# Layer 0 attention: the two turned scores of a step move to the end of TensorE's order

## The chip, the cores and the metric

The program runs on one NeuronCore of a Trainium2 chip. A core has a matrix engine (TensorE, PE in the rows; its weight loads are PEld), a vector engine (VectorE, DVE), a scalar engine (ScalarE, ACT), GpSimd (POOL) and SyncE (SP), which issues transfers. Each engine takes its own instructions in the order in which the program wrote them, and the engines meet only at semaphores. The metric is device microseconds (us) of one execution of the whole program; lower is better.

## The reference, cut to what matters

Two transformer layers, each an attention and a mixture of experts. The change is in the attention of layer 0 alone: four batches (B = 4) of 512 positions, width 256, 16 heads of 16.

```python
h = _layernorm(x) * (1 + ca) + sa
q, k, v = (proj(w, b) for each)                    # 16 heads of 16
q, k = _apply_rope(q, k, S)
scores = einsum('bhqd,bhkd->bhqk', q, k) / sqrt(16)
attn = softmax(scores, axis=-1)
ctx = einsum('bhqk,bhkd->bhqd', attn, v)
x = x + ga * (ctx.reshape(B, S, D) @ wo.T + bo)
```

## The kernel before, in words

Layer 0's attention (`attention0`) is one software pipeline. Its work is cut into 16 groups G (4 batches, 4 heads in each group), and the loop at the end of the function runs over steps s. In each step it writes what the five engines are to do, engine by engine: `tensor(s)`, `vector(s)`, `scalar(s)`, `gpsimd(s)`, `sync(s)`. That order is written out by hand, and each engine keeps it. A group takes eight steps for each of its parts, and the parts of successive groups overlap:

- **Row scores** (`tensor_scores`, L778): steps 8G to 8G+7. Two matmuls a step, one on rows 0 to 47 and one on rows 64 to 111 of the array. They fill a pair of banks (0 and 1, or 2 and 3). VectorE takes the row maxima (`vector_max`, L790) before the pair is used again two steps later.
- **The shift row**: at step 8G+8 GpSimd splits the maxima, at 8G+9 TensorE turns them (`tensor_nT`, L815, bank 7), at 8G+10 ScalarE copies them out (`scalar_nrow`, L824) and GpSimd issues four small transfers (`gpsimd_nmax`, L834) into rows 48 and 49 of the stack.
- **Turned scores** (`tensor_turned`, L854): steps 8G+13 to 8G+20 (EXP_AT = 13). Two matmuls a step (hh 0 and 1) into banks 4 and 5, each on 50 rows of one half of the array. ScalarE takes the exponential of each (`scalar_exp`, L869). The next step's turned score waits for it, since it uses the same bank.
- **Context** (`tensor_pv`, L883): every second step from 8G+16 (PV_AT = 16), eight matmuls of 32 columns into bank 6. VectorE turns and normalises the sum (L900, L905), GpSimd and ScalarE finish it (L910, L933, L939).
- **The shared bank.** Bank 7 serves everything else, one user at a time (`late = Banks(7, 1)`): the shift row (L815), the rows of the next batch (`tensor_rows`, L1068), its q and k (`tensor_qk`), its v (`tensor_v`), the output projection (`tensor_out`) and its way back (`tensor_back`, L466). The three matmuls of a split product are L126, L127 and L128. All these users fall on odd steps, and context on even steps.

A user of bank 7 first waits until the bank has been read out. Who reads it out, and when:

| user of bank 7 | steps | read out by, and where in that engine's order |
|---|---|---|
| `tensor_nT` | 8G+9 | ScalarE, L824, step + 1, behind that step's two exponentials |
| `tensor_qk`, odd half | 39, 47, 71, 79 | ScalarE, L663, step + 1, behind the exponentials |
| `tensor_v` | 19, 45, 59, 77, 91 | ScalarE, L735, step + 1, behind the exponentials |
| `tensor_rows` | 31, 35, 63, 67 | ScalarE, L1079, the same step, behind the exponentials |
| `tensor_qk`, even half | 43, 51, 75, 83 | VectorE, L674, step + 1, behind that step's maximum |
| `tensor_out` | 53, 55, 85, 87, 117, 119 | VectorE, L997, step + 1, behind the maximum |
| `tensor_back` | 61, 69, 93, 101, 125, 133 | VectorE, L478, step + 1, behind the maximum |

(Steps are those from 13 on, where there are exponentials.) The order of ScalarE within a step is set in `scalar`: first both exponentials, then the shift row, then everything else. ScalarE's halves of q and k (L689, L692) come at steps 45, 53, 77 and 85.

The q and k of a batch go out to DRAM and come back as stacks (SyncE L709, GpSimd L753). The stack of steps 64 to 79 is fetched at steps 51 and 58, and that of steps 96 to 111 at steps 83 and 90. In GpSimd's order the fetch of step 58 (and of 90) stands behind that step's L834.

Of the kernel before, what the change touches and what calls it, by code (L numbers as in the profile page):

```python
# [458 lines left out]
def tensor_residual(k, yT, half, bank, ready):  # L459

    pe, done = k.pe, k.sem("pe_yT")
    pe.wait_ge(*ready)
    for t in range(TT // 2):
        tile = half * (TT // 2) + t
        for i in range(KT):
            mm = pe.transpose(k.psum[:, bank, t * D + i * P:t * D + (i + 1) * P], yT[:, i, tile * P:(tile + 1) * P],  # L466
                              k.ident[:, :])
    mm.then_inc(done.sem, 1)
    return done.up()
# [18 lines left out]
def attention0(k):  # L488
# [7 lines left out]
    with ExitStack() as st:  # L496
# [146 lines left out]
        def tensor_qk(b, i, odd):  # L643
            qk_bank[b, i, odd] = n = g.next()
            if g.free[n]:
                pe.wait_ge(*g.free[n])
            pe.wait_ge(*norm.split_ready[b])
            if (b, odd) == (0, 1):
                pe.wait_ge(*stage_in[1 + i, "lo"])
            col = (2 * i + odd) * P  # L650
            for kt in range(KT):
                mm = k.mm3(psum[:, n, :], w(kt, col, col + P), norm.split(b, kt), kt == 0, kt == KT - 1)
            mm.then_inc(s_qk.sem, 1)
            qk_done[b, i, odd] = s_qk.up()
# [59 lines left out]
        def tensor_v(b, pair):  # L714
            v_bank[b, pair] = n = g.next()
            if g.free[n]:
                pe.wait_ge(*g.free[n])
            pe.wait_ge(*norm.split_ready[b])
            for j in range(2):
                t = 2 * pair + j  # L720
                for kt in range(KT):
                    mm = k.mm3(psum[:, n, j * D:(j + 1) * D], norm.split(b, kt, slice(t * P, (t + 1) * P)),
                               w(kt, 2 * D, 3 * D), kt == 0, kt == KT - 1)
            mm.then_inc(s_v.sem, 1)
            v_done[b, pair] = s_v.up()
            norm.split_free[0] = v_done[b, pair]
# [33 lines left out]
        def of(G, p):  # L760

            return stk[:, :, (G // 2) % NH, 2 * (G % 2) + p]

        def tensor_scores(G, r):
            p, qt = divmod(r, TT)
            u = 8 * G + r
            n = 2 * (u % 2)
            if u >= 2:
                pe.wait_ge(*max_done[u - 2])
            else:  # L770
                for bank in (n, n + 1):
                    pe.wait_ge(*g_first.free[bank])
            if r == 0:
                pe.wait_ge(*stk_in[G // 2])
            pair = of(G, p)
            for hh in range(2):
                rows = slice(64 * hh, 64 * hh + 48)
                mm = pe.matmul(psum[:, n + hh, :], pair[rows, 0, qt * P:(qt + 1) * P], pair[rows, 1, :], start=True,  # L778
                               stop=True)
            mm.then_inc(s_s.sem, 1)  # L780
            s_done[u] = s_s.up()
# [25 lines left out]
        def tensor_nT(G):  # L807
            nT_bank[G] = n = late.next()
            if late.free[n]:
                pe.wait_ge(*late.free[n])  # L810
            if G == 0:
                pe.wait_ge(*ident_r_ready)
            pe.wait_ge(*ncol_ready[G])
            for qt in range(TT):
                mm = pe.matmul(psum[:, n, qt * P:(qt + 1) * P], ncol[:, G % 2, qt, :], ident_r[:, :], start=True,  # L815
                               stop=True)
            mm.then_inc(s_nT.sem, 1)
            nT_done[G] = s_nT.up()
# [23 lines left out]
        def tensor_turned(G, r, hh):  # L842
            kt, p = divmod(r, 2)
            u = 2 * (8 * G + r) + hh
            if u >= 2:
                pe.wait_ge(*e_done[u - 2])
            else:
                pe.wait_ge(*g_first.free[4 + hh])
            if r == 0:
                pe.wait_ge(*nmax_in[G])  # L850
            if u == 0:
                pe.wait_ge(*ones_in)
            pair, rows = of(G, p), slice(64 * hh, 64 * hh + 50)
            pe.matmul(psum[:, 4 + hh, :], pair[rows, 1, kt * P:(kt + 1) * P], pair[rows, 0, :], start=True,  # L854
                      stop=True).then_inc(s_sT.sem, 1)
            sT_done[u] = s_sT.up()
            if G % 2 and r == 7:
                stk_free[G // 2] = sT_done[u]
# [13 lines left out]
        def tensor_pv(G, kt):  # L872
            b, gr = divmod(G, H0 // GROUP0)
            n = TT * G + kt
            if kt == 0:
                if G:
                    pe.wait_ge(*cT_done[G - 1])
                else:
                    pe.wait_ge(*g_first.free[6])
                pe.wait_ge(*v_ready[b])  # L880
            pe.wait_ge(*e_done[4 * n + 3])
            for j in range(GROUP0):
                mm = pe.matmul(psum[32 * j:32 * j + 32, 6, :], v[:, b % NV, kt, GROUP0 * gr + j, :],  # L883
                               et[:, n % NET, j, :], start=(kt == 0), stop=(kt == TT - 1),
                               tile_position=(0, 32 * j), skip_group_check=True)
            mm.then_inc(s_pv.sem, 1)
            pv_done[n] = s_pv.up()
# [99 lines left out]
        def tensor_last_back(half):  # L987
            y_bank[B - 1, half] = n = LAST_BACK[half]
            y_done[B - 1, half] = tensor_residual(k, oT, half, n, ot_done[B - 1])
# [69 lines left out]
        def tensor_rows(b, half):  # L1059
            h_bank[b, half] = n = late.next()  # L1060
            if late.free[n]:
                pe.wait_ge(*late.free[n])
            for t in range(2):
                at, ready = norm.xn_of[b, 2 * half + t]
                pe.wait_ge(*ready)
                for i in range(KT):
                    c = i * 2 * P + t * P
                    mm = pe.transpose(psum[:, n, c:c + P], norm.xn[:, at, i * P:(i + 1) * P], k.ident[:, :])  # L1068
                mm.then_inc(norm.s_xT.sem, 1)
                norm.xn_free[at] = h_turned[b, half] = norm.s_xT.up()  # L1070
# [36 lines left out]
        NCOL_AT, NT_AT, EXP_AT, PV_AT, CTX_AT = 8, 9, 13, 16, 23  # L1107
# [14 lines left out]
        def ahead(s, at):  # L1122

            for b in range(1, B):
                d = s - PER_BATCH * (b - 1) + (SOONER if b == 1 else 0)
                if d in at:
                    yield b, at.index(d)

        def groups(s, at, n=1, every=1):

            for G in range(NG):
                r, rest = divmod(s - 8 * G - at, every)
                if 0 <= r < n and rest == 0:
                    yield G, r

        def tensor(s):
            for G, r in groups(s, EXP_AT, 8):
                tensor_turned(G, r, 0)
            for G, r in groups(s, 0, 8):
                tensor_scores(G, r)  # L1140
            for G, r in groups(s, EXP_AT, 8):
                tensor_turned(G, r, 1)
            for G, kt in groups(s, PV_AT, TT, 2):
                tensor_pv(G, kt)
            for G, r in groups(s, NT_AT):
                tensor_nT(G)
            for b, half in ahead(s, ROWS_AT):
                tensor_rows(b, half)
            for b, j in ahead(s, QK_AT):
                tensor_qk(b, j // 2, 1 - j % 2)  # L1150
            for b, half in ahead(s, V_AT):
                tensor_v(b, half)
            for b in range(B):
                d = s - PER_BATCH * b
                if b < B - 1 and d in OUT_AT:
                    tensor_out(b, OUT_AT.index(d))
                if b < B - 1 and d in BACK_AT:
                    tensor_back(b, BACK_AT.index(d))
                for gr in range(GROUP0):
                    for m in range(KT):  # L1160
                        if b == B - 1 and d == LAST_OUT[gr][m]:
                            tensor_last_out(gr, m)
                if b == B - 1 and d == LAST_BACK_AT:
                    tensor_last_back(0)
                    tensor_last_back(1)

        def vector(s):
            for G, r in groups(s, 0, 8):
# [1850 lines left out]
def adaln_program(nc, ins, out):  # L3019
    with ExitStack() as stack:  # L3020
        k = Kernel(nc, ins, out, stack)
        begin(k)
        attention0(k)
        k.barrier()
        with ExitStack() as early:
# [108 lines left out]
```

## Time and profile before

| | us |
|---|---|
| median of three runs | 1456.45 |
| lowest and highest of them | 1448.93, 1463.96 |
| the profiled execution, whole time | 1450.06 |
| its span, first to last instruction | 1448.8 |
| of it layer 0's attention with turned scores, 70 to 335 | 265 |

### The profile page before, as it was taken

How to read it: one execution, taken by the hardware profiler on the slowest of the kernel's cores; microseconds unless marked ns; L12 is line 12 of the kernel's file. 1: busy time of each engine (PE TensorE's matmuls, PEld its weight loads, DVE VectorE, ACT ScalarE, POOL GpSimd, SP SyncE). 2: the span in 40 equal slices, each digit the busy share in tenths (PEclk: the TensorE clock that was granted, in tenths of full speed). 3: DMA queues.
4: the chain of work that ended last, by engine and by line, in shares of the span. 5: the costliest groups of instructions: out<-in, count | busy, mean ns of one | idle time of the engine just before them, and what ended most of it. 6: DMA issues, size and time to landing. Idle time of an engine off the chain costs nothing.

```text
span 1448.8 us, 22556 instructions
## 1 busy us (share of the span) xinstructions
PE 1294.8 (89%) x6461; PEld 913.3 (63%) x6461; DVE 874.5 (60%) x2649; ACT 780.0 (54%) x1907; POOL 441.0 (30%) x577
## 2 busy tenths in 40 slices
PE   6689799887889998799999999999999986999994
PEld 5334344334556776577777777787777764678773
DVE  5678687753553365765577566666676754543555
ACT  3267575653431545566666556665566643166562
POOL 5344545220344644200000006001410140455553
PEclk9689898987989999899999999999999997999997
DMA  6653617003213553144200001000100018555664
GB/s 219 135 123 84 154 31 151 2 2 149 107 49 99 162 163 100 36 143 140 69 1 1 16 1 60 1 16 1 45 16 16 1 44 326 186 158 156 209 192 139
DMA packets 79207, 133.99 MB, mean 92 GB/s; under 512 B 13788, under 2 KB 52708, under 8 KB 77420
## 3 DMA queue, kind: packets, MB, share of 16 engines
q1 hardware_dynamic: 62128, 92.39, 20.8%
q0 software_dynamic: 15712, 38.25, 9.4%
q10 hardware_dynamic: 1248, 1.90, 0.4%
q8 instruction: 57, 0.93, 0.3%
q14 instruction: 62, 0.51, 0.1%
HBM read 77.20 MB, written 60.00 MB: 95 GB/s over the span
## 4 chain that ended last, share of the span: by engine, by line
PE 69%; DVE 11%; issue 6%; DMA 6%; ACT 4%; POOL 4%; DVEq 0%; SPq 0%; ACTq 0%; POOLq 0%
PE psum L126 9%; PE psum L1984 8%; PE psum L128 8%; PE psum L127 8%; PE psum L2628 7%; PE psum L2674 4%; PE psum L1955 4%; PE psum L2501 4%; PE psum L854 3%; PE psum L883 3%; PE psum L2535 2%; PE psum L2597 1%; PE psum L778 1%; DVE a_nmax L790 1%; POOL slots L1635 1%
## 5 line engine op out<-in xcount | busy, mean ns | idle before, releaser
L790 DVE TENSOR_REDUCE a_nmax<-psum 128x2 f32<-128x1024 f32 x128 | 155.1, 1217 | 66.5 <-PE psum L778 65.5
L869 ACT ACTIVATE a_et<-psum 128x512 f32<-128x512 f32 x256 | 139.0, 594 | 92.0 <-PE psum L854 88.5
L1930 ACT ACTIVATE a_spare<-psum,a_nmax 128x128 f32<-128x128 f32 (+3 forms) x256 | 134.7, 526 | 93.4 <-DVE a_nmax L1919 87.6
L1919 DVE CUSTOM_DVE_ANT_0 psum<-psum,a_spare 128x128 f32<-128x128 f32 (+3 forms) x256 | 126.7, 495 | 79.4 <-PE psum L128 78.6
L2697 POOL DMA_INDIRECT results<-r_fin,r_to x134 | 134.3, 1002 | 123.0 <-ACT r_fin L2689 63.1
L1984 PE MATMUL psum<-a_et,a_v 128*128 128x512 f32 (+3 forms) x512 | 169.5, 433 | 0.0
L2628 PE MATMUL psum<-m_w,m_xT 128*128 x536 | 150.5, 403 | 0.0
L1964 ACT ACTIVATE a_et<-psum 128x128 f32<-128x128 f32 (+3 forms) x256 | 111.6, 436 | 64.2 <-PE psum L1955 60.7
L126 PE MATMUL psum<-a_kT,a_q 128*128 128x128 f32 (+3 forms) x256 | 118.9, 465 | 6.8 <-DVE a_q L1858 5.9
L854 PE MATMUL psum<-a_stk 50*128 50x512 f32 x256 | 109.0, 500 | 15.0 <-ACT a_et L869 12.1
L1955 PE MATMUL psum<-ident,a_spare 128*128 128x128 f32 x640 | 113.5, 275 | 0.6 <-DVE a_spare L1943 0.6
L2674 PE MATMUL psum<-m_w,m_hidT 128*128 (+1 forms) x346 | 103.1, 398 | 8.4 <-DVE m_hidT L2664 7.5
L1943 DVE TENSOR_SCALAR a_spare<-a_spare,a_rinv 128x128 f32<-128x128 f32 (+3 forms) x256 | 103.7, 405 | 9.0
L1984 PEld LDWEIGHTS psum<-a_et,a_v 128*128 128x128 f32 x512 | 95.6, 189 | 18.9
L1941 DVE RECIPROCAL a_rinv<-a_rsum 128x1 f32<-128x1 f32 x256 | 41.6, 163 | 107.7 <-ACT a_spare L1930 100.5
L854 PEld LDWEIGHTS psum<-a_stk 50*128 50x128 f32 x256 | 44.1, 201 | 98.2 <-ACT a_et L869 75.4
L778 PE MATMUL psum<-a_stk 48*128 48x512 f32 x256 | 96.5, 493 | 8.6 <-DMA a_stk<-stacks 6.7
L2645 DVE TENSOR_TENSOR m_hid<-m_silu,psum 128x128 f32<-128x128 f32 (+1 forms) x134 | 40.3, 300 | 103.8 <-ACT m_silu L2638 101.8
L2628 PEld LDWEIGHTS psum<-m_w,m_xT 128*128 128x128 f32 x536 | 91.4, 190 | 13.3
L2689 ACT ACTIVATE r_fin<-psum,r_to 128x256 f32<-128x256 f32 x134 | 63.2, 472 | 45.2 <-PE psum L2674 35.4
L128 PE MATMUL psum<-a_kT,a_q 128*128 128x128 f32 (+3 forms) x256 | 83.7, 327 | 0.0
L1955 PEld LDWEIGHTS psum<-ident,a_spare 128*128 128x128 f32 x640 | 76.7, 141 | 10.9 <-issue 2.4
(326 smaller groups left out, 2940.6 us busy)
## 6 DMA issues: line engine op xcount, KB each, us to landing
r_xs<-slots SPq DMA_DIRECT2D x134, 129.0 KB, 2.3
slots<-empty SPq DMA_DIRECT2D x12, 1290.0 KB, 6.6
m_w<-in_experts SPq DMA_DIRECT2D x16, 768.0 KB, 14.3
stacks<-a_qk SPq DMA_DIRECT2D x32, 256.0 KB, 3.8
a_stk<-stacks POOLq DMA_DIRECT2D x32, 256.0 KB, 7.0
r_shared_hid<-results SPq DMA_DIRECT2D x12, 512.0 KB, 4.6
m_w<-in_experts SPq DMA_DIRECT2D x4, 1216.0 KB, 14.2
a_stk<-stacks POOLq DMA_DIRECT2D x32, 128.0 KB, 6.3
```

Source lines behind the costliest of these rows:

```text
L126: self.pe.matmul(out, lh, rh, start=start, stop=False, skip_group_check=True)
L128: return self.pe.matmul(out, ll, rh, start=False, stop=stop, skip_group_check=True)
L790: dve.tensor_reduce(nmax[:, G % 2, qt, 2 * p:2 * p + 2], psum[:, n:n + 2, :], AX.X, ALU.max, negate=True).then_inc(s_max.sem, 1)
L854: pe.matmul(psum[:, 4 + hh, :], pair[rows, 1, kt * P:(kt + 1) * P], pair[rows, 0, :], start=True, stop=True).then_inc(s_sT.sem, 1)
L869: act.activation(et[:, n % NET, 2 * p + hh, :], psum[:, 4 + hh, :], ACT.Exp).then_inc(s_e.sem, 1)
L1919: dve.tensor_tensor_reduce(psum[:, n, 0:W], psum[:, n, 0:W], mask[:, S - W:S], 1.0, BIG, ALU.add, ALU.min, nmax[:, u % NE, :]).then_inc(s_ ...
L1930: act.activation(e[:, u % NE, 0:W], psum[:, n, 0:W], ACT.Exp, bias=nmax[:, u % NE, :], scale=-1.0, accum_out=rsum[:, u % NE, :]).then_inc( ...
L1955: mm = pe.transpose(psum[:, n, c:c + P], e[:, u % NE, kt * P:(kt + 1) * P], k.ident[:, :])
L1984: mm = pe.matmul(psum[:, n, kt * P:S], v[:, b % 2, kt, h // HPG1 * HD1:(h // HPG1 + 1) * HD1], queries(i, kt), start=(kt == 0), stop=(kt = ...
L2628: mm = pe.matmul(psum[:, n, 0:2 * hid], xT[:, i % NT3, j, :], w[:, bass.ds(start_of[i] + j * 2 * hid, 2 * hid)], start=(j == 0), stop=(j = ...
L2674: mm = pe.matmul(psum[:, n, 0:D], hdT[:, i % NT2, c, :], w[0:CH, bass.ds(start_of[i] + KT * 2 * hid + c * D, D)], start=(c == 0), stop=(c ...
L2697: pool.indirect_dma_start(results[:, :], bass.IndirectOffsetOnAxis(ap=to[:, i % NI, 0:1].bitcast(U32), axis=0), ys[:, o, :], None, bounds_ ...
```

## The change

In `tensor(s)` the two turned scores no longer stand ahead of and behind the row scores. Both are issued at the very end of the step, behind the context and behind whatever uses the shared bank.

```diff
         def tensor(s):
-            for G, r in groups(s, EXP_AT, 8):
-                tensor_turned(G, r, 0)
             for G, r in groups(s, 0, 8):
                 tensor_scores(G, r)
-            for G, r in groups(s, EXP_AT, 8):
-                tensor_turned(G, r, 1)
             for G, kt in groups(s, PV_AT, TT, 2):
                 tensor_pv(G, kt)
             for G, r in groups(s, NT_AT):
...
                 if b == B - 1 and d == LAST_BACK_AT:
                     tensor_last_back(0)
                     tensor_last_back(1)
+            for G, r in groups(s, EXP_AT, 8):
+                tensor_turned(G, r, 0)
+                tensor_turned(G, r, 1)
```

No instruction is added or taken away. The orders of the other four engines, the steps of all parts and every semaphore's count stay as they are.

## Rows read from the trace of the kernel before

**Rows 1.** The page, part 1: busy time, share of the span, instructions, each engine
```profile
PE 1294.8 (89%) x6461; PEld 913.3 (63%) x6461; DVE 874.5 (60%) x2649; ACT 780.0 (54%) x1907; POOL 441.0 (30%) x577
```

**Rows 2.** Stretches: bounds, us, PE, PEld, DVE, ACT, POOL busy, clock, DMA share, GB/s
```profile
70.00:335.00 265.00, 236.92 (x1291) 104.75 (x1292) 185.57 (x220) 170.81 (x320) 105.64 (x180) 0.90 0.34 77
...
186.00:240.00 54.00, 52.53 (x316) 25.54 (x314) 43.48 (x46) 38.31 (x73) 26.38 (x42) 1.00 0.35 89
...
257.00:306.00 49.00, 41.89 (x249) 17.93 (x249) 37.77 (x41) 30.60 (x58) 13.07 (x24) 1.00 0.01 2
```

**Rows 3.** Waits of TensorE, 84 to 310 us: total, times, longest
```profile
PE psum L854 <- ACT a_et L869: 7.4, 15, 0.7
PE psum L778 <- DMA a_stk<-stacks: 6.7, 2, 6.3
```

**Rows 4.** Timeline of steps 78 and 79: start, length, engine, line, count, idle before
```profile
205.38 0.50 PE L854 MATMUL psum<-a_stk 50*128 50x512 f32 x1
205.38 0.72 PE L778 MATMUL psum<-a_stk 48*128 48x512 f32 x2
205.91 1.08 ACT L869 ACTIVATE a_et<-psum 128x512 f32<-128x512 f32 x2 [0.21 <-PE psum L854]
206.05 1.06 PE L883 MATMUL psum<-a_et,a_v 128*32 128x512 f32 x8
207.05 0.50 PE L854 MATMUL psum<-a_stk 50*128 50x512 f32 x1
207.18 0.60 ACT L735 ACTIVATE a_v<-psum 128x512 f32<-128x512 f32 x1 [0.19 <-PE psum L883]
207.83 0.51 PE L126 MATMUL psum<-h_hi_a,a_w_hi 128*128 128x512 f32 x1
209.43 0.49 PE L854 MATMUL psum<-a_stk 50*128 50x512 f32 x1
```

**Rows 5.** Groups by line on ScalarE, 70 to 335 us: busy, mean ns, idle before
```profile
L869 ACT ACTIVATE a_et<-psum 128x512 f32<-128x512 f32 x256 | 139.0, 594 | 92.0 <-PE psum L854 88.5
L824 ACT ACTIVATE a_nrow<-psum 8x512 fp32r<-8x512 f32 x15 | 8.5, 569 | 0.0
L1079 ACT ACTIVATE h_a<-psum,mod 128x256 f32<-128x256 f32 x8 | 4.1, 566 | 0.5 <-PE psum L1068 0.4
L689 ACT ACTIVATE a_qk<-a_turned 128x512 fp32r<-128x512 f32 x5 | 3.2, 633 | 0.0
L735 ACT ACTIVATE a_v<-psum 128x512 f32<-128x512 f32 x5 | 3.0, 602 | 0.4 <-PE psum L883 0.4
L663 ACT ACTIVATE a_turned<-psum,a_bias 128x512 f32<-128x512 f32 x4 | 2.8, 692 | 0.0
```

**Rows 6.** Timeline of steps 107 to 109, where bank 7 has no user
```profile
265.41 0.49 PE L854 MATMUL psum<-a_stk 50*128 50x512 f32 x1
266.65 0.49 PE L854 MATMUL psum<-a_stk 50*128 50x512 f32 x1 [0.50 <-ACT a_et L869]
267.56 1.06 PE L883 MATMUL psum<-a_et,a_v 128*32 128x512 f32 x8
269.16 0.46 PE L854 MATMUL psum<-a_stk 50*128 50x512 f32 x1 [0.53 <-DMA a_stk<-a_nrow]
```

**Rows 7.** Timeline: the first matmul of step 58
```profile
159.44 0.49 PE L854 MATMUL psum<-a_stk 50*128 50x512 f32 x1
```

**Rows 8.** The chain that ended last, from step 58 to step 64: start, length
```profile
161.81 2.10 POOL a_stk L834 x4
...
165.39 11.35 DMA a_stk<-stacks
176.88 0.80 PE psum L778 x2
```

**Rows 9.** Busy time by stretch, as in rows 2, ahead of and behind a clock fall
```profile
239.00:243.00 4.00, 3.07 (x18) 0.97 (x16) 3.85 (x6) 2.65 (x5) 4.00 (x9) 1.00 1.14 223
243.10:256.70 13.60, 13.29 (x53) 4.97 (x52) 7.33 (x8) 6.99 (x13) 4.36 (x8) 0.50 0.56 80
```

## The prediction

> **What bounds the kernel now.** I read the page first. TensorE is busy for 89% of the span, the next engine for 60% [rows 1]. Then the stretches: in layer 0's attention TensorE is busy for 236.92 of 265 us, and in its crowded part, 186 to 240, for 52.53 of 54 at full clock [rows 2]. There VectorE has 43.48 and ScalarE 38.31, so neither can be the bound by its amount of work. From 257 to 306, where no next batch is being prepared, TensorE still has 41.89 of 49 [rows 2]. Third, TensorE's waits: from 84 to 310 us its matmuls wait 7.4 us for exponentials and 6.7 us for stacks, 6.3 of it once [rows 3]. So the stage runs as fast as TensorE works its list off, and every new wait in that list lengthens it unless it falls into a wait that is there anyway.
>
> Last, the timeline, for how a step fits together [rows 4]. Step 78 begins at 205.38 with turned and row scores. The row scores start with the first turned score, so two matmuls on the two halves of the array run side by side. The four take 0.67 us (205.38 to 206.05). Context starts at 206.05 and takes 1.00 us (to 207.05). Step 79's four take 0.67 again, and then the shared bank's user, q of the next batch, starts at 207.83. Two steps with such a user: 209.43 - 205.38 = 4.05 us.
>
> **The change part by part.** Nothing is added or removed, so matmul time changes by nothing. Read in a ring, the order is turned, scores, context, turned, scores, shared user in both kernels: the turned scores of step s now lie next to the row scores of s + 1 instead of those of s. They can still pair (two on one half, two on the other), and there are as many changes between kinds of matmul. Bounds for this: a gain of nothing, since the four already take two slots [rows 4], and a loss of nothing, since each half still has two matmuls. I take 0.
>
> What does change is what the turned scores are behind. ScalarE keeps its order: in step s + 1 first both exponentials, then the read-out of bank 7 that the user of step s filled. Before, the turned scores of s + 1 stood at the head of the step, and the read-out was over by the time that TensorE had done context and the next four: L735 ran from 207.18 to 207.78, and L126 started at 207.83, 0.05 later and at most 0.1 us after it could have [rows 4]. Now these turned scores stand behind context. Let T be when they start. The exponentials start at T + 0.53 (205.91 - 205.38) and take 1.08 [rows 4]. The read-out takes 0.57, 0.60 or 0.69 (L824, L735, L663) [rows 5]. With 0.05 to hand over, the bank is free at T + 0.53 + 1.08 + 0.60 + 0.05 = T + 2.26. TensorE has only the row scores to do beside the turned ones and is at the bank's next user at T + 0.67. The gap is 1.59; an activation begins some 0.1 before the last one ends (two of 0.594 take 1.08), so I take **1.5 us for each user of bank 7 that comes two steps after one read out by ScalarE**. Queued behind the waiting user are the turned scores of its step and the next row scores, hence ScalarE and VectorE as well: nobody catches up for it. A user read out by VectorE costs nothing new: its maximum depends on row scores, and between these and the next user stands the same work as before.
>
> On how strictly TensorE keeps its order: in rows 4 nothing passes L126 while the bank is still being read, which alone doesn't show that nothing could. The Trainium skill ("TensorE: Matmul & The Clock Gate", Architectural detail) says that this engine's queue pulls weight loads ahead but no matmuls. By that rule the sum below stands whole. If turned scores could pass the waiting user, the stalls would go and the time stay as it was.
>
> The sum, with the steps of the users:
>
> - Full stalls at 41, 43, 47, 49, 51 and at 73, 75, 79, 81, 83: 10 x 1.5 = 15.0.
> - At 45 and 77 ScalarE also has halves of q to make (L689 and its twin, 0.63 each [rows 5]), now ahead of the next exponentials and the bank behind them. Up to 1.2 each; half is hidden by context. 2 x 0.6 = 1.2.
> - Stalls at 19, 35, 67. Two of them run at half clock, where TensorE's own work covers more. Between 0.9 and 1.5; 3 x 1.2 = 3.6.
> - After rows of the next batch (33, 65, 69): read out in the same step by two activations of 0.566 [rows 5], free at T + 0.53 + 1.08 + 1.0 = 2.6 against a next user at 0.67 + 1.00 + 0.67 = 2.34. 3 x 0.24 = 0.7.
> - Steps 58 to 64. The row scores of 64 wait for a stack whose fetch stands on GpSimd behind L834, which follows step 58's exponentials: 159.44 to 176.88, 17.4 us [rows 7, 8]. This chain goes on being the limit, so the two stalls at 59 and 61 fall into it and cost nothing. But it now starts one row scores and one context later: 0.67 + 1.00 = 1.7.
> - Steps 90 to 96, the same chain with only a 0.4 us wait at its end (6.7 - 6.3 [rows 3]). Two stalls, 3.0, less that: 2.6.
> - Odd steps without a user (14 of them, most after step 95). Two steps of scores run on end there, limited by exponentials: from one turned score to the next 1.24 us, and 0.91 instead of 0.67 until context [rows 6]. The second turned score is what waits. Row scores now stand behind it instead of ahead: one slot more, 0.24. 14 x 0.24 = 3.4.
>
> Together 15.0 + 1.2 + 3.6 + 0.7 + 1.7 + 2.6 + 3.4 = **28.2 us**.
>
> The shift row's transfers have 1.0 us less cover (one context), and step 109's turned score already waits 0.53 for them [rows 6]. Between 0 and 1.0 for each of the 5 late groups; I take 0: three delays of 0.24 us in each group, already counted, and the later start of the turned scores themselves give most of that cover back.
>
> **The clock.** A stretch with TensorE busy for 3.07 of 4 us was followed by 13.6 us at 0.50, that is 1.2 GHz [rows 9]. Such a stretch costs: 53 matmuls in 13.6 us, against 249 in 49 us or 69 in 13.6 at mostly full clock [rows 2, 9], so 13.6 x (1 - 53/69) = 3.1 us. With stalls, TensorE is busy for about 4.05 of 5.55 us in the crowded part, which is a lower share. How often that makes the clock fall no row tells: 0 to 5 times. I take half a fall, 1.6, as a stall between dense matmuls isn't a long rest. Sum: 28.2 + 1.6 = 29.8.
>
> After the attention everything waits for its result, so the 29.8 us reach the end. The tail (steps 129 to 142) doesn't change: context no longer waits behind turned scores, the last exponentials come as before.
>
> **The rivals.**
>
> *Same, within 1% (0.12).* ScalarE's read-out is late but TensorE's list had slack, or later matmuls pass the waiting one, and only the 3.4 + 1.7 us and a few stalls are left: +0 to +14, some 1460. For it: 7.4 + 6.7 us of waits to fall into [rows 3]. Against it: in the crowded part TensorE idles for only 1.5 of 54 us [rows 2].
>
> *Much slower (0.14).* The ten stalls follow each other, and the clock falls in them: 3 to 6 falls of 3.1 us on top, +39 to +47, some 1497. For it: rows 9. Against it: at half clock TensorE's own 0.67 becomes about 1.2 us and the stalls shrink by the difference.
>
> *Faster (0.03).* The second turned score used to stand behind row scores, which may wait for a maximum or a stack. Now the turned ones go first, and exponentials run through that wait. It would have to take most of 7.4 + 6.7 = 14.1 us [rows 3] and hence give at best 1439. It decides only if ScalarE's read-outs aren't waited for, so if the bank were free by T + 0.67; L126's 0.05 us behind L735 speaks against that [rows 4].
>
> *Forecast (0.71).* Slower by some 30 us.
>
> **How the numbers follow.** 1450.06 + 29.8 = 1479.9 for an execution like the profiled one. The median of the runs shown is 6.4 higher; I go half way, 3.2, and predict 1483. Low end: half of the 28.2 on the profiled time, 1464. High end: the median, 29.8 and five falls, 1456.4 + 29.8 + 15.5 = 1502. Within 1% (14.6 us) is about what a measurement can tell from no change. Slower by over 1%: 0.71 + 0.14 = 0.85. Within 1%: 0.12. Faster by over 1%: 0.03.
>
> **What would show it.** Right: matmuls of bank 7's users (L815, L126, L1068, L466) wait for L824, L735 and L663, about 1.5 us each and some 20 us in all; the attention takes 265 + 30 = 295 us; two steps such as 78 and 79 take 5.5 instead of 4.05; the wait for the stack at step 64 is about 6.3 + 1.7 - 3.0 = 5.0 us. Everything behind the attention keeps its length. Wrong: no waits for ScalarE at bank 7 (then exponentials aren't as late as said), waits of 1.5 us with the attention hardly longer (then another chain was the limit), or more than five stretches at 0.50 in the attention (then the clock is the term that was missed).

## The result, and the profile after

The changed kernel takes 1499.16 us (median of four runs, 1490.23 to 1503.83) against 1456.97 for the kernel before. The ratio is 1.0287, with an interval from 1.0250 to 1.0323: slower by 2.9%. The prediction was 1483, between 1464 and 1502, slower. The direction and the main mechanism hold. The time lies only 3 us below the high end of the range, and the loss of 42 us is well above the 26 that 1483 stood for; in the profiles it is 40.1 against 29.8, a third more.

The profiled execution spans 1488.9 us, 40.1 more than that of the kernel before. These are the stretches of the changed kernel from 45 us on. The columns are the bounds in us, the length, the busy time (and instructions) of PE, PEld, DVE, ACT and POOL, TensorE's granted clock, the transfers' share and GB/s. The second line is layer 0's attention, from the first exponential to the last context:

```profile
45.00:68.50 23.50, 17.98 (x72) 10.34 (x71) 17.95 (x18) 5.02 (x8) 7.02 (x12) 0.86 0.43 98
68.50:367.50 299.00, 249.23 (x1284) 107.49 (x1284) 184.45 (x218) 168.26 (x318) 104.62 (x178) 0.87 0.29 66
367.50:493.80 126.30, 106.75 (x434) 72.35 (x426) 64.63 (x306) 39.23 (x85) 40.23 (x43) 0.83 0.28 103
493.80:1234.00 740.20, 696.64 (x3516) 543.75 (x3516) 459.45 (x1576) 436.44 (x1159) 152.31 (x196) 0.98 0.17 53
1234.00:1488.90 254.90, 215.68 (x1036) 161.92 (x1036) 123.19 (x459) 114.17 (x313) 110.57 (x111) 0.93 0.60 192
```

The same stretches of the kernel before:

```profile
72.00:334.30 262.30, 235.49 (x1286) 104.23 (x1286) 183.61 (x217) 168.82 (x318) 104.67 (x178) 0.90 0.33 76
334.30:460.00 125.70, 104.71 (x434) 71.54 (x427) 63.76 (x307) 39.58 (x85) 40.23 (x43) 0.85 0.28 103
460.00:1200.00 740.00, 694.88 (x3516) 542.81 (x3516) 461.19 (x1576) 436.54 (x1159) 152.17 (x196) 0.99 0.17 53
1200.00:1448.80 248.80, 214.01 (x1036) 160.94 (x1036) 122.69 (x458) 114.25 (x313) 110.69 (x111) 0.93 0.62 197
```

The attention grew by 299.0 - 262.3 = 36.7 us. The two stretches behind it kept their length to within 0.6 us, so the loss goes on to the end whole. The last stretch is 6.1 us longer and the attention began 3.5 us sooner. From the last score matmul of layer 1 to the end it is 274.5 us here and 268.5 before; in the other kernels of this study, one profile of each, it lies between 267.2 and 273.6. The three kernels with TensorE's order of before have 268.1 to 269.2; of the nine with another order eight have more (271.1 to 274.5) and one less (267.2). So it is open whether a part of the 6.1 us goes with the moved order, and nothing shows by what way. It can't be much of the time: with ScalarE's order turned round as well (first experiment), the moved order is as fast as the kernel before.

Now TensorE's longest waits in the attention of the changed kernel, from 70 us on (who waited for whom, total, times, longest):

```profile
PE psum L126 <- ACT a_nrow L824: 9.1, 7, 1.4
PE psum L854 <- DMA a_stk<-a_nrow: 9.0, 5, 4.8
PE psum L815 <- ACT a_turned L663: 5.8, 4, 1.5
PE psum L854 <- ACT a_et L869: 5.7, 13, 0.7
PE psum L126 <- ACT a_v L735: 3.5, 2, 1.8
PE psum L778 <- DMA a_stk<-stacks: 3.2, 1, 3.2
PE psum L466 <- ACT a_v L735: 2.7, 2, 1.4
PE psum L1068 <- ACT a_nrow L824: 2.6, 2, 1.4
```

Five of the eight rows are users of bank 7 that wait for ScalarE's read-out: 9.1 + 5.8 + 3.5 + 2.7 + 2.6 = 23.7 us in 17 waits, 1.39 each. In the kernel before no matmul at bank 7 shows such a wait; its longest rows were those of [rows 3]. The 17 places are those that the prediction names: the ten full stalls, the three at 19, 35 and 67, two in steps 58 to 64, two in steps 90 to 96.

And this is one of them, the same steps 78 and 79 as in [rows 4] (start, length, engine, line, count, idle before; rows between these are left out):

```profile
223.58 0.50 PE L854 MATMUL psum<-a_stk 50*128 50x512 f32 x2
224.24 1.06 PE L883 MATMUL psum<-a_et,a_v 128*32 128x512 f32 x8
225.23 0.57 PE L854 MATMUL psum<-a_stk 50*128 50x512 f32 x2
225.66 0.63 ACT L692 ACTIVATE a_qk<-a_turned 128x512 fp32r<-128x512 f32 x1
226.18 1.08 ACT L869 ACTIVATE a_et<-psum 128x512 f32<-128x512 f32 x2
227.14 0.62 ACT L735 ACTIVATE a_v<-psum 128x512 f32<-128x512 f32 x1
227.81 0.50 PE L126 MATMUL psum<-h_hi_a,a_w_hi 128*128 128x512 f32 x1 [1.77 <-ACT a_v L735]
```

The turned scores of step 78 start at 225.23, behind context. The exponentials follow at 226.18 (here the halves of q are in the way as well), L735 ends at 227.76, and L126 starts 0.05 later, 1.77 us after TensorE could have. Nothing overtakes it. From the turned scores at 223.58 to the next ones of an odd step's end, at 229.63, two steps take 6.05 us instead of the 4.05 of [rows 4].

### The profile page after: what moved, and what is told of

Read it like the earlier page. It is cut to its first block, busy times and chain, and to the rows that moved or that the text cites. A ratio compares the mean times of both kernels' runs of the same rounds, so it can differ in the third digit from the quotient of the medians.

```text
span 1488.9 us, 22556 instructions
## 1 busy us (share of the span) xinstructions
PE 1311.8 (88%) x6461; PEld 917.7 (62%) x6461; DVE 873.1 (59%) x2649; ACT 778.6 (52%) x1907; POOL 442.0 (30%) x577
## 4 chain that ended last, share of the span: by engine, by line
PE 68%; DVE 10%; issue 7%; DMA 6%; ACT 4%; POOL 3%; another core or an unknown queue 1%; SPq 0%; DVEq 0%; POOLq 0%; ACTq 0%
PE psum L126 9%; PE psum L1983 8%; PE psum L128 8%; PE psum L127 8%; PE psum L2627 6%; PE psum L2673 4%; PE psum L1954 4%; PE psum L854 4%; PE psum L883 3%; PE psum L2500 3%; PE psum L2534 2%; PE psum L778 1%; PE psum L2596 1%; ACT a_et L869 1%; DVE a_nmax L790 1%
## 5 line engine op out<-in xcount | busy, mean ns | idle before, releaser
L126 PE MATMUL psum<-a_kT,a_q 128*128 128x128 f32 (+3 forms) x256 | 119.2, 465 | 6.7 <-DVE a_q L1857 5.8
L854 PE MATMUL psum<-a_stk 50*128 50x512 f32 x256 | 85.8, 550 | 15.8 <-DMA a_stk<-a_nrow 9.0
L854 PEld LDWEIGHTS psum<-a_stk 50*128 50x128 f32 x256 | 34.9, 203 | 102.7 <-ACT a_et L869 72.9
L2673 PEld LDWEIGHTS psum<-m_w,m_hidT 128*128 128x128 f32 (+1 forms) x346 | 57.2, 190 | 43.4 <-issue 35.8
```

What stands on the lines that cost most here:

```text
L126: self.pe.matmul(out, lh, rh, start=start, stop=False, skip_group_check=True)
L2673: mm = pe.matmul(psum[:, n, 0:D], hdT[:, i % NT2, c, :], w[0:CH, bass.ds(start_of[i] + KT * 2 * hid + c * D, D)], start=(c == 0), stop=(c ...
```

## Experiments

Theory A: the loss comes from ScalarE's order. Its read-outs of bank 7 stand behind exponentials that now come one context later. Rivals: B, that transfers and the clock make the loss; C, that any place behind bank 7's user is bad; D, that the new neighbours in TensorE's order lose the pairing on the two halves of the array; E, that the long wait for the shift row is only its late copy. "Above before" below is the ratio less 1, times 1453 us, about the median of the kernel before beside these runs.

### Read-outs ahead of the exponentials

```diff
         def scalar(s):
+            for G, r in groups(s, NT_AT + 1):
+                scalar_nrow(G)
+            for b, i in ahead(s, (QK_AT[0] + 1, QK_AT[2] + 1)):
+                scalar_rope(b, i)
+            for b, half in ahead(s, tuple(d + 1 for d in V_AT)):
+                scalar_v(b, half)
             for G, r in groups(s, EXP_AT, 8):
                 scalar_exp(G, r, 0)
                 scalar_exp(G, r, 1)
```

The three loops are gone from where they stood.

> The changed kernel, but in ScalarE's order of a step the three kinds of read-out of bank 7 that belong to the step before (L824 shift row, L663 rope, L735 v) stand ahead of the two exponentials. TensorE's order is that of the changed kernel. Theory A (the read-out waits behind exponentials that are now late): the waits of bank 7's users for ScalarE, 23.7 us in the changed kernel, shrink to under 4 us, and the time comes back to 3 to 12 us above the kernel before. Rival B (transfers and the clock make the loss, and the read-outs only happen to be what ended the waits): the other engines stay late, and the time stays at least 25 us above the kernel before.

Measured: 1449.89 us, ratio 0.9985 (0.9961 to 1.0009), so 2 us below the kernel before, with 1 inside the interval. Its TensorE waits:

```profile
PE psum L854 <- ACT a_et L869: 8.6, 18, 0.8
PE psum L778 <- DMA a_stk<-stacks: 5.4, 1, 5.4
...
PE psum L126 <- ACT a_v L735: 1.6, 2, 0.8
```

Of the 23.7 us, 1.6 are left. They are at steps 47 and 79, where the halves of q are still ahead of L735. TensorE's order was not touched, so the loss of 2.9% hung on what ScalarE did first, and what the order costs by itself is too small for these times to show. Rival B falls: transfers and the clock came back with the stalls (the attention takes 260.5 us, from first exponential to last context). Theory A expected 3 to 12 us too many even then, of which 3.4 were for steps that run on end. That cost is smaller: from context to context around step 107, where no transfer is waited for, it is 3.32 us here and in the changed kernel, against 3.15 in the kernel before.

### Only the shift row's copy ahead

```diff
         def scalar(s):
+            for G, r in groups(s, NT_AT + 1):
+                scalar_nrow(G)
             for G, r in groups(s, EXP_AT, 8):
                 scalar_exp(G, r, 0)
                 scalar_exp(G, r, 1)
-            for G, r in groups(s, NT_AT + 1):
-                scalar_nrow(G)
```

> The changed kernel with only the copy of the shift row (L824) ahead of the exponentials on ScalarE. Theory A: the waits for L824 (9.1 + 2.6 us in the changed kernel) go, those for L663 and L735 (5.8 + 6.2) stay, so 10 to 16 us less than the changed kernel, 24 to 30 above the kernel before. The shift row's transfers are also issued earlier, so the wait of turned scores for them (9.0 us) shrinks by up to 6 if it was lateness, and stays if it is contention with the filling of slots. Rival B: no more than 3 us less.

Measured: 1467.95 us, ratio 1.0097 (1.0067 to 1.0126): 14 us above before, 28 below the changed kernel. I had expected 24 to 30 above. The mechanism held, and these are rows of its waits:

```profile
PE psum L815 <- ACT a_turned L663: 5.9, 4, 1.5
...
PE psum L126 <- ACT a_v L735: 3.6, 2, 1.8
PE psum L466 <- ACT a_v L735: 2.7, 2, 1.4
```

L824 is gone from the list, while the others stand as they were (12.2 us). But the gain was over twice its 11.7 us: the wait of turned scores for the shift row's transfers, 9.0 us, went to nothing too. In the profile the attention takes 277.3 us, 21.7 less than in the changed kernel, which is about these two waits. L824 is ahead of both, the bank and four transfers.

### Behind bank 7's user, ahead of context

```diff
+            for G, r in groups(s, EXP_AT, 8):
+                tensor_turned(G, r, 0)
+                tensor_turned(G, r, 1)
+            for G, kt in groups(s, PV_AT, TT, 2):
+                tensor_pv(G, kt)
```

These stand at the end of `tensor(s)`, in this order, and nowhere else: in a step neither context nor turned scores stand ahead of bank 7's user any longer.

> The turned scores stand behind row scores and behind bank 7's user, but ahead of context. A half of the change: passed on odd steps, not passed on even ones, where exponentials must come soon for the read-out. Theory A (it is context, on the even steps, that must not come first): the exponentials of an even step start some 0.4 us after its row scores, the bank is free at about 2.26 us against a user at 2.0, so a wait of 0.3 us or less for each; 2 to 9 us above the kernel before. Rival C (any place behind bank 7's user is bad): above 20 us.

Measured: 1503.18 us, ratio 1.0319 (1.0259 to 1.0379), 46 us above before. My expectation of 2 to 9 was badly off, though bank 7 behaves as said: its users wait for ScalarE for 1.1 us in all. The loss is elsewhere:

```profile
PE psum L854 <- ACT a_et L869: 29.4, 59, 0.8
...
PE psum L126 <- ACT a_v L735: 1.1, 2, 0.6
```

And two steps of its timeline, with a user of bank 7 (L815) on the odd one:

```profile
191.24 0.50 PE L778 MATMUL psum<-a_stk 48*128 48x512 f32 x2
191.67 0.66 PE L815 MATMUL psum<-a_ident_r,a_ncol 128*128 128x128 f32 x4
192.26 0.50 PE L854 MATMUL psum<-a_stk 50*128 50x512 f32 x2
193.50 0.99 PE L854 MATMUL psum<-a_stk 50*128 50x512 f32 x2 [0.51 <-ACT a_et L869]
194.42 1.06 PE L883 MATMUL psum<-a_et,a_v 128*32 128x512 f32 x8
195.41 0.50 PE L778 MATMUL psum<-a_stk 48*128 48x512 f32 x2
```

The odd step's turned scores come last and the even step's right after its row scores, so only one slot of row scores lies between them. But 1.24 us must (192.26 to 193.50, the same 1.24 as in [rows 6]), since the banks are free only after the exponentials. Behind both there is context and a user of bank 7, where turned scores would have had room. Two steps take 4.17 us; in the kernel before, two with the same user took 3.16 (262.25 to 265.41). In the changed kernel context or bank 7's user lies between two steps' turned scores, but for the odd steps without a user.

### The same, with the read-outs ahead

This is the run above with the edit to `scalar(s)` of the first experiment.

> Turned scores behind bank 7's user and ahead of context, as in the run that came out some 50 us above the kernel before, now with ScalarE's read-outs of bank 7 ahead of the exponentials. Theory F (that run lost its time to exponentials: on even steps its turned scores come only one slot of row scores behind those of the odd step, and 1.24 us must lie between two steps' turned scores): no gain from the read-outs, 35 to 55 us above the kernel before, with the waits of turned scores for exponentials still at about 30 us. Theory A alone (bank 7's read-out): under 15 us above the kernel before.

Measured: 1507.88 us, ratio 1.0393 (1.0348 to 1.0439), 57 us above before, with this wait:

```profile
PE psum L854 <- ACT a_et L869: 28.8, 59, 0.8
```

The read-outs gave nothing here (the expected 35 to 55 was a little low). So this order's loss isn't bank 7's, and rival C falls: a place behind bank 7's user is harmless in the first experiment and costs 3 to 4% here. What counts is the distance between two steps' turned scores.

### Behind context, ahead of bank 7's user

Turned scores stand here and nowhere else:

```diff
             for G, kt in groups(s, PV_AT, TT, 2):
                 tensor_pv(G, kt)
+            for G, r in groups(s, EXP_AT, 8):
+                tensor_turned(G, r, 0)
+                tensor_turned(G, r, 1)
             for G, r in groups(s, NT_AT):
                 tensor_nT(G)
```

> The other half: the turned scores stand behind row scores and context, but ahead of bank 7's user. Theory A: on even steps the exponentials are as late as in the changed kernel. The next step's turned scores now fill part of the wait, but they are bound to the exponentials themselves (1.24 us from one to the next), so that bank 7's user still comes at about 2.3 us instead of 2.34 minus context's 1.0: 15 to 30 us above the kernel before. Rival C: under 8 us.

Measured: 1516.95 us, ratio 1.0441 (1.0392 to 1.0491), 64 us above before, more than twice what I expected. Its largest wait is again the one for exponentials, 24.0 us in 57 waits, with the mirror image of the order above: here the odd step's turned scores follow the even step's with one slot between. The expectation priced that distance as something that fills the stall; it is a loss of its own in every pair of steps, also where bank 7 has no user.

### Both turned scores first

```diff
         def tensor(s):
             for G, r in groups(s, EXP_AT, 8):
                 tensor_turned(G, r, 0)
+                tensor_turned(G, r, 1)
             for G, r in groups(s, 0, 8):
                 tensor_scores(G, r)
-            for G, r in groups(s, EXP_AT, 8):
-                tensor_turned(G, r, 1)
```

> The kernel before with both turned scores at the head of the step, ahead of the row scores: the same neighbours as in the changed kernel (turned, turned, row, row in one run), without the move behind context and bank 7's user. Theory A: the pairing on the two halves of the array stays, only the steps that run on end lose a slot of 0.24 us: 0 to 4 us above the kernel before. Rival D (the order of the four itself costs, by lost pairing): each of 128 steps loses a slot of 0.33 us, and the time is over 15 us higher.

Measured: 1452.13 us, ratio 0.9996 (0.9962 to 1.0029). The neighbours of the changed kernel cost nothing that these times show, to within 5 us either way. Rival D, which asked for over 15 us, falls, and the prediction's 0 for pairing stands.

### The changed kernel with the fillings moved

The slots of the expert layer are filled with zeros by four transfers of 1.29 MB (the last 1.16) from SyncE. In the changed kernel the turned scores of step 37 waited 4.8 us for the shift row. Its chain there (start, length, what):

```profile
110.81 1.58 POOL a_stk L834 x3
112.39 5.94 DMA a_stk<-a_nrow
118.46 0.89 PE psum L854 x2
```

and SyncE's filling at step 36, first in the changed kernel, then in the kernel before, beside GpSimd's issue of the shift row's transfers in the latter:

```profile
111.93 0.38 SPq L195 DMA_DIRECT2D slots<-empty  x1
```

```profile
113.28 2.10 POOL L834 DMA_DIRECT2D a_stk<-a_nrow  x4 [1.88 <-ACT a_nrow L824]
...
115.22 0.38 SPq L195 DMA_DIRECT2D slots<-empty  x1
```

The filling now starts 1.1 us after the first of the four small transfers, where it used to start 1.9 us after, behind all four. The trace tells what that did to each: the two issued at 110.81 and 111.37 landed in 1.64 and 1.59 us, the third, 0.05 us ahead of the filling, in 4.32, and the fourth, 0.46 us behind it, in 5.94. In the kernel before all four landed in 1.59 to 1.65. The edit moves the four fillings to steps where neither they nor a stack is on the way:

```diff
-            j, rest = divmod(s - 12, 24)
-            if rest == 0 and 0 <= j < len(k.fills) and k.fills[j][0] == 0:
-                fill_slots(k, j, s_done[s])
+            if s in (14, 38, 70, 102):
+                fill_slots(k, (14, 38, 70, 102).index(s), s_done[s])
```

> The changed kernel with the four fillings of the slots (1.29 MB each) issued at steps 14, 38, 70 and 102 instead of 12, 36, 60 and 84, so that none is under way together with the shift row's transfers of steps 10 to 13 of a group or with the stack's fetch ahead of steps 64 and 96. Theory A with contention as its second term: the wait of 4.8 us at step 37 shrinks to about 1.5, that at step 64 (3.2) goes; 4 to 9 us less than the changed kernel, 31 to 38 above the kernel before. Rival E (the 4.8 us are only the lateness of the copy L824): no more than 1 us less.

Measured: 1489.26 us, ratio 1.0244 (1.0193 to 1.0294), 35 us above before and 6 below the changed kernel by the ratios, though the two intervals overlap. The profile decides it. Its wait for the shift row:

```profile
PE psum L854 <- DMA a_stk<-a_nrow: 4.1, 4, 1.3
```

The 9.0 us became 4.1 and the longest wait 1.3 instead of 4.8, the wait for the stack at step 64 (3.2 us) is gone, and the attention takes 290.8 instead of 299.0 us. So the long wait was contention with the filling (rival E falls). The other four waits stay at their steps and at their size (29, 101, 109 and 125, 0.7 to 1.3 us each); they are the lateness of L824, since the copy ahead took them to nothing in the second experiment.

### The fillings moved in the kernel before, and all edits together

The same four lines in the kernel before; then in the run with turned scores last and read-outs ahead; then in the kernel before with read-outs ahead.

> The kernel before with the same four fillings moved. If the 11.35 us that the stack's fetch takes ahead of step 64 are contention with the filling that starts 0.3 us after it, the wait of 6.3 us there shrinks by 3 to 6 us, and the kernel is 3 to 8 us faster than before (the clock's fall behind that wait may go too). If the fetch takes that long by itself, no difference.

> Turned scores last, ScalarE's read-outs of bank 7 ahead of the exponentials, and the fillings moved: all that was found put together. By theory A the stalls are gone, and the wait for the stack at step 64 (5.4 us with the read-outs ahead) goes as well: 5 to 12 us faster than the kernel before. Rival: the wait for the stack is set by GpSimd's order, not by the filling, and it is within 3 us of the run with the read-outs ahead.

> The kernel before (TensorE's order untouched) with ScalarE's read-outs of bank 7 ahead of the exponentials and the four fillings of the slots moved. If TensorE's order in itself is neutral, this is within 3 us of the same two edits on top of the changed order (ratio 0.9942): 5 to 12 us faster than the kernel before. If the changed order gives something that the late read-out had covered (turned scores ahead of row scores that wait), this is 4 us or more behind that one.

| | median us | ratio to before | interval | attention in the profile |
|---|---|---|---|---|
| fillings moved | 1449.76 | 0.9955 | 0.9921 to 0.9989 | 259.9 |
| and turned scores last, read-outs ahead | 1446.29 | 0.9942 | 0.9914 to 0.9970 | 250.1 |
| and read-outs ahead, TensorE's order as before | 1440.42 | 0.9955 | 0.9928 to 0.9983 | 250.3 |

(The first two medians and the third come from different sets of runs; each ratio is to the kernel before of its own set.) The second row's kernel is faster than both kernels of this case, by 0.6%. In it TensorE's matmuls wait neither for a stack nor, but for 0.2 us, for the shift row, and the clock stays up:

```profile
70.30:320.40 250.10, 231.73 (x1280) 101.80 (x1284) 182.98 (x217) 167.75 (x319) 105.10 (x178) 0.96 0.36 79
```

The three ratios can't be told apart, and the attention takes the same 250 us in both orders of TensorE. So turned scores last give nothing by themselves, and by the ratios most of the gain is the fillings'. By how much the read-outs add to it these runs don't settle: the attentions say 10 us, the ratios nothing, and the granted clock (0.90 with the fillings alone, 0.96 here) is a part of the 10. The read-outs ahead alone, in TensorE's order of before, were not run. In the run with the fillings alone the 6.7 us of waits for stacks [rows 3] shrank to 0.7 and yet the attention got only 2.4 us shorter: waits for the shift row rose from 2.2 to 5.0 us, with two new ones of 1.7 us at steps 69 and 101; why they came is open.

## Why the prediction was right, and where it was short

**The mechanism.** It named the queue (ScalarE's exponentials ahead of the read-out), the places and the price of one stall. Seventeen waits of 1.39 us on average came, against 1.5 in the sum. With the queue's order turned round the loss is gone. The turned scores don't pass the waiting matmul: at steps 78 and 79 TensorE stands still for 1.77 us, though the exponential that frees bank 4 for the next turned score was over at 226.78, 1.03 us before L126 started. The Trainium skill ("TensorE: Matmul & The Clock Gate", Step-by-step: what each phase is for) says that the queue pulls weight loads ahead while matmuls keep the program's order, and by that rule the sum was the right one. As a rule for every matmul the trace of the kernel before contradicts it: in 113 of the 128 steps the second matmul of the row scores, the one that signals their semaphore, starts ahead of the first, which uses the other half of the array (205.39 against 205.72 us in step 78). So what is shown here is that nothing passed a matmul that waits for its bank, and the waiting ones of bank 7 take all 128 rows of the array.

**The sum, stretch by stretch.** The table takes the start of the row scores (L778) of a step in both profiles and shows how the difference grows between two steps.

| steps | forecast, without the clock | measured | what the trace shows |
|---|---|---|---|
| 12 to 32 | 2.2 | -1.0 | 7 us less at half clock at the start |
| 32 to 40 | 1.7 | 7.0 | the filling in front of the shift row, step 37 |
| 40 to 58 | 8.1 | 9.6 | the row of stalls |
| 58 to 64 | 1.7 | -0.7 | chain 2 us shorter from L834 on (below) |
| 64 to 84 | 9.8 | 14.1 | the second row of stalls, more at half clock |
| 84 to 96 | 2.8 | 1.9 | |
| 96 to 104 | 0.5 | -3.0 | the clock's fall of [rows 9] is missing |
| 104 to 116 | 1.0 | 4.7 | half clock instead |
| 116 to the last context | 0.5 | 3.7 | |

**The terms that were mis-sized.**

- *The shift row's transfers, taken at 0.* They cost 9.0 - 2.2 = 6.8 us. The prediction saw the 1 us of lost cover, gave a range of 0 to 1 for each of five groups and chose the low end, on the grounds that other delays give the cover back; they didn't. And it didn't look at what else SyncE's queue would send in that moment. Moving the fillings gives 4.9 us back, the copy ahead gives all.
- *The clock, taken at 1.6.* The granted clock of the attention is 0.87 against 0.90. At 0.50, that is 1.2 GHz, it runs for 77 us against 55, so 22 us more. At the prediction's own price (3.1 us in 13.6) they cost 5.1 us, an estimate. In the crowded part, where TensorE is the bound, the price is probably higher; no run isolates it. One of the prediction's own signs of being wrong came: more than five stretches at 0.50 in the attention. There are nine, of 1.9 to 20.5 us, against four of 13.6 before. This stretch is mostly at 1.2 GHz:

```profile
298.00:319.00 21.00, 20.48 (x70) 8.97 (x70) 9.96 (x10) 8.44 (x16) 4.36 (x8) 0.53 0.01 2
```

- *The 3.4 us of steps that run on end.* The cost is real but was put too high. From context to context at full clock it is 3.15 us around steps 27 and 107 in the kernel before and 3.34 and 3.32 here, 0.17 to 0.19 more and not 0.24; around steps 23 and 103, where context waits for VectorE, it is 3.67 and 3.73 before and 3.68 and 3.74 here. By that it is under 2 us in all, an estimate. The 0.7 us for rows of the next batch shouldn't have been there: no matmul waits for L1079.
- *The halves of q.* They were put at 0.6 us each behind the users at 45 and 77. What they cost is at the next users, 47 and 79: waits of 1.76 and 1.77 us against 1.39 on average.
- *Steps 58 to 64.* The stack's chain went on being the limit, and the two stalls fell into it, as predicted. It starts 1.3 us later in the step, not 1.7 (from the first row scores of step 58 to L834 3.7 us against 2.4), and this was made good: in [rows 8] 15.1 us lie from L834 to the row scores of step 64, here 13.0 (L834 at 175.65, scores at 188.66), as the stack's transfer in the chain took 9.30 us instead of 11.35. The wait is 3.2 us, against 5.0 forecast.

By waits: 23.7 us at bank 7, 6.8 more for the shift row, 3.5 less for stacks (6.7 to 3.2) and 5.4 less of turned scores for exponentials (12.1 to 6.7, the first steps included) make 21.6 of the 36.7 us. The rows of the stretches say the same in another way. TensorE's idle time in the attention grew from 26.8 to 49.8 us, by 23.0; the other 13.7 are busy time (235.49 to 249.23) of the same matmuls. Against the run with the read-outs ahead, which has the very same order on TensorE, busy time is 12.0 us longer (237.21 there) with 35 us more at half clock. So a large part of the 13.7 is probably the clock, more than the 5.1 at the prediction's price, and a part are the steps that run on end; how it divides is not shown.

**The rivals.** "Much slower" was half right. By its number the result belongs to it: +40 us in the profile, in its +39 to +47, and 1499 us against its 1497. The clock did fall more often too, but in shorter falls, by 22 us of half clock over the stage, which is under two of the falls of 13.6 us and not 3 to 6; and a part of the loss is the wait for the shift row, which is in neither sum. That the range still holds the result is in part luck: its high end has five falls in it, and what took their place was other terms. "Faster" had its mechanism too, fewer waits of turned scores (12.1 to 6.7 us), under a larger loss.

## What to carry to other kernels

When instructions move within one engine's order, write down for every other engine what is queued behind the result that now comes later. Here it was a 0.6 us copy behind two exponentials, and it cost 2.9%; turning that engine's own order round made the move free, as far as the times can tell. A result that two things wait for (L824: a bank and four transfers) pays twice. And where an engine-to-engine loop has a least distance (from one step's turned scores to the next some 1.2 us, and in no kernel here under 1.14), any order that leaves less work than that between two of them loses in that turn: the two orders that did so cost 3.2 and 4.4%.

## What I had not expected of the hardware

A transfer of two rows of 2 KB took 5.94 us to land, where its like in the kernel before took 1.62, when it was issued 0.46 us behind a transfer of 1.29 MB on another queue. One issued 0.05 us ahead of the large one took 4.32. TensorE's half clock came without any long rest: it fell in the changed kernel's attention at about 298 us, where no wait of a matmul in the 36 us ahead was longer than 1.4 us, and the engine had been busy for 30.1 of the 36. And two matmuls on different halves of the array can start in the other order than the program's, by 0.33 us, as told above.
